# Triangle inversion in a gated delta-rule kernel: one chain of dependent VectorE steps split into two, over even and over odd rows

## What is computed

```python
def step(state, inp):
    q_t, k_t, v_t, a_t, b_t = inp
    pred = jnp.einsum('bhde,bhd->bhe', state, k_t)
    error = v_t - pred
    update = jnp.einsum('bhe,bhd->bhde', b_t[..., None] * error, k_t)
    state = a_t[..., None, None] * state + update
    out = jnp.einsum('bhde,bhd->bhe', state, q_t)
    return (state, out)
_, ys = lax.scan(step, state0, (qt, kt, vt, at, bt))
...
x = x + 0.5 * _L0_ffn_ref(_layernorm(x, axis=-1), ...)
x = x + _L0_attn_ref(_layernorm(x, axis=-1), ...)
x = x + 0.5 * _L0_ffn_ref(_layernorm(x, axis=-1), ...)
```

## Time and profile before

| What | Value |
|---|---|
| Runs | 2969.35, 2973.77, 2973.11 us; median 2973.11 us |
| Span of the profiled execution | 2958.8 us, 117088 instructions |
| Own time of the profiled execution | not recorded beside its span; the median of the runs is 14.3 us above the span |
| Busy | PE 91%, PEld 65%, DVE 64%, ACT 36%, POOL 45% |
| Granted TensorE clock | 0.985 of full speed in the mean |
| Transfers | 224.78 MB, mean 76 GB/s |

### The profile page before, as it was taken

One profiled execution on the slowest core, in us unless ns is written; L12 is line 12 of the kernel. 1 busy time (PEld: TensorE's weight loads), 2 busy tenths in 40 slices (PEclk: granted clock), 3 DMA queues, 4 the chain that ended last, 5 costly groups with the idle time before them and its releaser, 6 DMA issues. The chain is left out here.

```text
span 2958.8 us, 117088 instructions
## 1 busy us (share of the span) xinstructions
PE 2700.6 (91%) x51052; PEld 1927.0 (65%) x51052; DVE 1882.3 (64%) x5306; ACT 1059.9 (36%) x1964; POOL 1328.6 (45%) x1767
## 2 busy tenths in 40 slices
PE   7999889899999999999999999999999999999867
PEld 5887556566666666666666666666666666666653
DVE  6777456566666666666666666666666666665626
ACT  5777223333333333333333333333333333333220
POOL 2222444445545444444554545555554444455410
PEclk9999999999999999999999999999999999999988
DMA  7352112211122222212222222212222222122178
GB/s 234 94 162 65 42 49 61 59 49 46 56 60 61 61 61 61 60 56 54 58 58 58 60 61 59 57 49 54 58 58 61 61 61 61 54 55 60 46 250 309
DMA packets 365965, 224.78 MB, mean 76 GB/s; under 512 B 277584, under 2 KB 294032, under 8 KB 365456
## 3 DMA queue, kind: packets, MB, share of 16 engines
q1 hardware_dynamic: 356240, 200.51, 24.0%
q10 hardware_dynamic: 9216, 16.78, 1.5%
HBM read 125.49 MB, written 74.97 MB: 68 GB/s over the span
## 5 line engine op out<-in xcount | busy, mean ns | idle before, releaser
L899 PE MATMUL psum<-w_all,xnT 128*128 128x512 f32 (+2 forms) x2048 | 732.6, 501 | 41.5 <-DVE xh L3297 33.9
L2602 POOL TENSOR_TENSOR sm<-sm,half 128x1 f32<-128x1 f32 (+1 forms) x384 | 535.3, 1394 | 85.1 <-ACT sm L2149 69.1
L899 PEld LDWEIGHTS psum<-w_all,xnT 128*128 128x128 f32 x2048 | 372.2, 190 | 285.7 <-issue 235.5
L3269 DVE TENSOR_TENSOR blk<-blk 128x30 f32<-128x30 f32 (+14 forms) x960 | 382.3, 398 | 33.0
L3267 DVE TENSOR_TENSOR blk<-blk 128x30 f32<-128x30 f32 (+14 forms) x960 | 369.8, 385 | 40.0 <-issue 14.2
L954 PE MATMUL psum<-xnT,w_all 128*128 128x128 f32 x2048 | 264.4, 281 | 0.9 <-DVE xc L3168 0.9
L1069 PE MATMUL psum<-pk,uw 32*32 32x64 f32 x8192 | 221.6, 216 | 44.3 <-issue 44.2
L1101 PE MATMUL psum<-w_out,gate 128*128 128x512 f32 x512 | 253.0, 613 | 5.4 <-DVE gate L3291 3.6
L954 PEld LDWEIGHTS psum<-xnT,w_all 128*128 128x128 f32 x2048 | 245.4, 193 | 16.6 <-issue 6.3
L1060 PE MATMUL psum<-pk,uw 32*32 32x64 f32 x8192 | 226.4, 221 | 24.9 <-issue 23.0
L1060 PEld LDWEIGHTS psum<-pk,uw 32*32 32x32 f32 x8192 | 141.6, 104 | 116.6 <-issue 101.3
(11 more groups left out here) (278 smaller groups left out, 4662.6 us busy)
## 6 DMA issues: line engine op xcount, KB each, us to landing
blk<-n_scratch SPq DMA_DIRECT2D x64, 512.0 KB, 4.4
xin<-in_L_attn_x_dram SPq DMA_DIRECT2D x96, 256.0 KB, 2.8
xh<-xc SPq DMA_DIRECT2D x64, 256.0 KB, 2.3
n_scratch<-nn SPq DMA_DIRECT2D x64, 256.0 KB, 3.6
e_scratch<-blk SPq DMA_DIRECT2D x32, 512.0 KB, 2.6
E<-e_scratch SPq DMA_DIRECT2D x64, 256.0 KB, 3.2
x_scratch<-xh SPq DMA_DIRECT2D x62, 256.0 KB, 2.3
rxn<-in_L_attn_x_dram SPq DMA_DIRECT2D x32, 256.0 KB, 3.0
```

Of the source, the lines that this page charges most:

```text
L899: last = mm(dst, xnT[b][:, k * P:(k + 1) * P], w_all[:, k * WK + at:k * WK + at + n], start=(k == 0), stop=(k == KC - 1))
L2602: return g.tensor_tensor(dst, a, half[:, 0:n], ALU.pow)
L3269: ins = tt(Y[:, 0:rows, s_ + 1:CH], Y[:, 0:rows, s_ + 1:CH], o, ALU.add)
```

## The change

`invert` splits the rows 0 to s - 1 of each step into the even ones and the odd ones, by a row stride of 2. Each half has its own product and its own sum. The two products of a step are issued first, into two halves of `outer` (offsets 0 and 128), then the two sums. `own.mark` gives an instruction its increment and returns the number, without a wait; `own.until` waits for such a number. The product of a half waits for the sum of the same half in the step before, and the sum of a half for its product. A wait that stood behind an instruction now stands in front of the one that needs it. In step 1 there is one row, and so one half.

```diff
@@ -239,6 +239,14 @@
                 ins.then_inc(self.sem, 1)
                 self.n += 1
                 self.e.wait_ge(self.sem, self.base + self.n)
+
+            def mark(self, ins):
+                ins.then_inc(self.sem, 1)
+                self.n += 1
+                return self.base + self.n
+
+            def until(self, count):
+                self.e.wait_ge(self.sem, count)
@@ -3254,6 +3262,8 @@
+            turned_rows = [0, 0]
+
             def invert(n, first, last):
@@ -3262,15 +3272,22 @@
                 for s_ in range(first, last):
-                    rows, cols = s_, CH - 1 - s_
-                    o = outer[:, 0:rows * cols].rearrange("p (r t) -> p r t", r=rows)
-                    own(tt(o, Y[:, 0:rows, s_:s_ + 1].to_broadcast([P, rows, cols]),
-                           N[:, s_:s_ + 1, s_ + 1:CH].to_broadcast([P, rows, cols]), ALU.mult))
-                    ins = tt(Y[:, 0:rows, s_ + 1:CH], Y[:, 0:rows, s_ + 1:CH], o, ALU.add)
-                    if s_ < CH - 2:
-                        own(ins)
-                    else:
-                        ins.then_inc(inv, 1)
+                    cols = CH - 1 - s_
+                    halves = [(h, (s_ + 1 - h) // 2) for h in range(2) if (s_ + 1 - h) // 2 > 0]
+                    products = []
+                    for h, rows in halves:
+                        o = outer[:, h * P:h * P + rows * cols].rearrange("p (r t) -> p r t", r=rows)
+                        if s_ > 1 + h:
+                            own.until(turned_rows[h])
+                        products.append((o, own.mark(tt(o, Y[:, h:s_:2, s_:s_ + 1].to_broadcast([P, rows, cols]),
+                                                        N[:, s_:s_ + 1, s_ + 1:CH].to_broadcast([P, rows, cols]), ALU.mult))))
+                    for (h, rows), (o, made) in zip(halves, products):
+                        own.until(made)
+                        ins = tt(Y[:, h:s_:2, s_ + 1:CH], Y[:, h:s_:2, s_ + 1:CH], o, ALU.add)
+                        if s_ == CH - 2 and h == 1:
+                            ins.then_inc(inv, 1)
+                        else:
+                            turned_rows[h] = own.mark(ins)
```

## The result

The changed kernel takes 3022.93 us (median of 4 runs, 3015.18 to 3034.48), the kernel before on the same chip 2973.44 us (4 runs, 2969.35 to 2973.79). The ratio is 1.0171, with a 95% interval of 1.0144 to 1.0197: slower by about 50 us, where the prediction had 27 us less. The profiled execution took 3020.4 us with a span of 3018.2 us, 59.4 us more than the span before.

The account below looks back on a forecast made before the run. TensorE, busy 91%, was taken as limited where it stands still for late VectorE work, VectorE not being the bound. Shorter `xh` waits (23 us) plus edges (4 us) gave 27 us: 2973.1 - 27 = 2946 us, range 2928 to 2976 us.

Parts of the forecast that it names:

- rival C: Overlapping VectorE instructions leave GpSimd no turn until the piece ends; TensorE's norm comes 2.6 us later: 3003 us, chance 0.11.
- The overlap: Inversion instructions on VectorE that needn't wait for their neighbour start before it ends: 2.9 us less per inversion.
- the fixed part: VectorE's cost per overlapping instruction besides 1.04 ns an element: 0.07 us, the middle of readings 0.09 and 0.05.
- Rival B: No overlap on VectorE: each half instruction costs the dependent 0.21 us + 1 ns an element; 3330 us, chance 0.04.
- both pass after `qa`: Step 15's two sums on VectorE pass in the turn after `qa`; TensorE's wait for `xh` goes: 1.21 us a step.
- `slotacc` comes between them: GpSimd's `slotacc` runs between step 15's two sums; `second_sum` ends at 1552.6 in place of 1553.15: 0.6 us a step.
- the sum's main term: TensorE's wait for `xh`, behind `second_sum` on VectorE, gets 0.93 us shorter in each of 25 steps: 23 us.
- rival A: GpSimd's turns hold `second_sum` where it is; the 1.21 us wait for `xh` stays 1.2: 2971 us, chance 0.15.
- what lies around the span: Time of a run outside the profiled span, 14.3 us from the median of the runs; the change doesn't touch it.

Follow-up runs that it names:

- e6: The changed kernel, but the first product of each step waits for both sums of the step before: 2981.64 us, ratio 1.0007 to the kernel before.
- e4: The changed kernel with the same 118 instructions, each waiting for the one right in front, so nothing overlaps: 3237.61 us, ratio 1.0943 to the kernel before.
- e2: The changed kernel with steps 10 to 15 of the inversion as one unsplit chain, all others split: 2954.97 us, ratio 0.9987 to the kernel before.
- e11: The changed kernel with steps 10 to 12 as one unsplit chain, all others split: 2965.73 us, ratio 0.9957 to the kernel before.
- e3: The changed kernel with GpSimd's two `sq` additions replaced by memsets, which read nothing: 2904.98 us, ratio 0.9817 to the kernel before.
- e9: The changed kernel with steps 10 to 12 as one unsplit chain and `slotacc` moved later on GpSimd: 2939.06 us, ratio 0.9879 to the kernel before.
- e1: The changed kernel, with VectorE waiting in step 12 until GpSimd has finished `sq`: 2959.98 us, ratio 0.9991 to the kernel before.
- e10: The changed kernel with only `slotacc` moved later on GpSimd, behind `qa`: 3040.29 us, ratio 1.0203 to the kernel before.
- e5: The kernel before, inversion untouched, with four small GpSimd powers delaying `sq` of batch 1: 3094.47 us, ratio 1.0398 to the kernel before.

## Why the prediction was wrong

**The step that failed** is the one in rival C's "against it": "when both queue, the rows show strict turns, one instruction each, and the turns are now shorter". Those rows were of dependent instructions, with 0.03 us between one's end and the next one's start. With such a gap the turn came every time. Where instructions overlap it is no longer sure: GpSimd's `sq` waited through some 15 of them, 3.54 us, while `qa` and `pk` still got theirs at once. The two places stood side by side in the prediction, the gap in C's first sentence and the turns in its last, and I gave the second the greater weight: 0.11 for what came true. C itself says too much: it has GpSimd as a whole without a turn. That the one instruction that TensorE's norm waits for was the one held off, no row of before could tell. e6 and e4 show it from one side (the same instructions with gaps, `sq` at most 850 and 733 ns), e2 and e11 from the other (wide dependent instructions, 895 ns at most), and e3 that it concerns `sq` as a read and not as a write.

**What held.** The overlap: the pair of step 11, 120 and 100 elements, takes 0.37 us to the next (1566.72 to 1567.09), 0.19 each. By 1.04 ns an element that leaves 0.07 us as the fixed part, the value that I had taken. It was luck in part, since it was the middle of two readings, and the reason that I gave for not trusting the first, that having waited lengthens an instruction, hardly shows: 120 elements take 0.27 us overlapping and 0.28 us in e4, 30 elements 0.19 us in both. Rival B was rightly small, and its price of 3330 us was of the right kind: e4, which is B made by hand, is 9.4% slower, some 275 us, where I had 360. The Trainium skill, VectorE: DVE Perf Modes, section "The DRAIN you can't avoid", has the next operation wait until the pipeline is empty, adds that one which isn't held back starts earlier, and says that chaining without semaphores gains nothing. The trace agrees that an operation can start earlier and disagrees on the semaphores: these start 0.19 us apart when neither waits for its neighbour and 0.31 us apart when each does (e4, 1511.99 to 1512.61 for two).

**That `xh` was the place.** The wait for `xh` was what the split could shorten, and the steps in front of it are what it shortens. That is shown by e3 and e9, in which it is gone. The middle between "both pass after `qa`" and "`slotacc` comes between them", 0.93 us (0.9 by its own two ends, 1.21 and 0.6), was wrong even apart from `sq`: as soon as `sq` is let in, `qa` and `slotacc` come one behind the other, and the second takes the turn after a single half instruction (e1's 2.39 us for two products). e11, with steps 10 to 12 unsplit, still waits 28.0 us of the 30.3 us: 2 us gained at this wait where the sum had 23. (e11 is some 13 us faster all the same; where the other 11 us come from was not traced.) So the sum's main term needed `slotacc` to move as well, and rival A was under-rated too; it would have been the case right behind C.

**C's size.** C said 2.6 us of wait per step and 3003 us. The wait measured 2.85 us; its 35 us net of 1.4 us per step came out as 38 us (68.6 - 30.3). Some 22 us are the granted clock of 0.50 behind 13 of the 25 stalls, a term that C hadn't got. Before has no stall of that length in its steady stretch, and its 1.21 us wait leaves the clock at 1.00, but its clock does fall behind a pause of 1.63 us (the 0.70 of 1520 to 1525 us above). So the term could have been seen, and I should at least have kept it in C as an open end.

**Around the span.** I took 14.3 us for what lies around the span, from the median of the runs. The changed kernel's profiled execution shows 2.2 us (3020.4 - 3018.2). If it was 2.2 us before too, the profiled execution of before took some 2961 us and was a quick one, 12 us under the median. That doesn't touch the difference forecast, since I only subtracted.

**The range.** 2928 to 2976 us left C outside with its 0.11. With the gap and the turns weighed as they deserved it should have been a case of the first rank, and the range should have reached beyond 3003 us. (Its lower end is mis-added: 2935 less 10 is 2925, not 2928.)

## What to carry to other kernels

When instructions of an engine are made to overlap, the gaps between them go, and with them whatever another engine did in these gaps: look for each GpSimd instruction that reads SBUF beside the piece and price it twice, at one turn (what `qa` and `pk` got) and at the length of the whole piece (what `sq` got); where the second would hurt, leave a few dependent instructions exactly where it is due. Where an engine waits between two of another's instructions and each turn lets one instruction pass, make the instructions at that place large, not small. A stall of TensorE that grows from 1.2 to near 3 us costs more than its length, since the work behind it may run at half the clock.

## What the runs showed of the hardware that was not expected

- **Overlapping VectorE instructions with two SBUF inputs can keep a reading GpSimd instruction out** for as long as they follow one another: 3.54 us for one of 0.72 us. The Trainium skill, SBUF — State Buffer, section "Who interferes with whom", has the lock between the two engines held for one instruction. The trace agrees for dependent instructions (`sq` 726 ns in e2, at most 891), in that a write alone isn't held (304 to 319 ns in e3), and for `qa` and `pk` among overlapping ones (at most 1.09 and 1.12 us); for `sq` it goes further, as if the lock passed from one VectorE instruction to the next.
- **What picks out `sq` is open.** A difference that the trace shows is the moment. In each of the 25 steps with a stall `sq` starts 4 to 34 ns before VectorE's next instruction does, while the `qa` of L2682 starts 81 to 86 ns before it. In the first and last tiles `sq` itself meets overlapping instructions at 78 ns or more before the next one's start five times, and takes 0.74 to 0.83 us. But e10 has two that were held off at 72 and 81 ns, so the moment isn't the whole rule, and no run shifts `sq` by itself.
- **A turn can go to half an instruction.** In e1 `slotacc` came in behind `qa` after one half instruction. Two GpSimd instructions one behind the other cost two halves of a pair 2.39 us.
- **TensorE's clock after a stall.** Behind the stalls of 2.85 us the granted clock fell to 0.50 in 13 of 25 steps and stayed at 1.00 in 12, with the same work before and after. Behind the 25 stalls of 3.6 us in e5 it fell each time. Behind the 25 waits of 1.21 us of before it never did, though it fell at four other places. What decides between the 13 and the 12 isn't settled.
